# First attention: scores seven quarters ahead in place of eight, maxima rows by one transfer, another order of the first steps

## The reference

```
x = x + L0_attn(layernorm(x))     # 16 heads of 8, differential: x1 - lv*x2, softmax(q k / sqrt 8) v
x = x + L0_ffn(layernorm(x))      # 8 experts, top 2, capacity, 512 wide
x = x + L1_attn(layernorm(x))     # 16 heads of 64, causal, batches of 256
x = x + L1_ffn(layernorm(x))      # 8 experts, top 4, 64 wide, and a shared one
```

## Time and profile before

| | |
|---|---|
| timed runs, median | 1486.77 us (1484.62 to 1487.56) |
| profiled execution | 1496.64 us, span 1495.1 us |
| busy, share of span | PE 96%, DVE 72%, ACT 64%, POOL 50% |
| chain that ended last, by engine | PE 79%, DVE 10%, ACT 5%, issue 2%, POOL 1%, DMA 1% |
| POOL's idle time ahead of `land` (L2441) | 97.0 us, of it 92.2 for the DMA to `dm` |

### The profile page before, as it was taken

One profiled execution on the slowest core, in us unless ns is written; L12 is line 12 of the kernel. 1 busy time (PEld: TensorE's weight loads), 2 busy tenths in 40 slices (PEclk: granted clock), 3 DMA queues, 4 the chain that ended last, 5 costly groups with the idle time before them and its releaser, 6 DMA issues.

```text
span 1495.1 us, 26269 instructions
## 1 busy us (share of the span) xinstructions
PE 1438.5 (96%) x8801; PEld 854.5 (57%) x8801; DVE 1074.0 (72%) x3430; ACT 950.1 (64%) x2448; POOL 744.3 (50%) x1260
## 2 busy tenths in 40 slices
PE   4999999999989999999999999999999999999999
PEld 2434443444437889974565565656565565655666
DVE  5899999999953677647667777777768777674433
ACT  4588888887874333436767777676767767674221
POOL 7434556655554653535636455463636544343322
PEclk9999999999999999999999999999999999999999
DMA  7366655456434565730000000000000000021331
GB/s 136 63 156 134 141 143 147 104 111 150 120 118 149 184 215 183 257 114 15 15 1 14 3 7 11 1 15 2 15 2 9 7 1 2 1 51 37 71 77 51
DMA packets 70601, 113.39 MB, mean 76 GB/s; under 512 B 18858, under 2 KB 35115, under 8 KB 70459
## 3 DMA queue, kind: packets, MB, share of 16 engines
q0 software_dynamic: 33104, 61.73, 17.0%
q1 hardware_dynamic: 36928, 49.19, 11.1%
q10 hardware_dynamic: 434, 0.79, 0.2%
HBM read 71.86 MB, written 39.91 MB: 75 GB/s over the span
## 4 chain that ended last, share of the span: by engine, by line
PE 79%; DVE 10%; ACT 5%; issue 2%; POOL 1%; DMA 1%; ACTq 0%; DVEq 0%; POOLq 0%
PE pS L1396 10%; PE bank L1429 9%; PE bank L1409 8%; PE bank L1240 6%; PE pS L1211 4%; DVE mx L1836 4%; PE bank L1438 4%; PE bank L1381 4%; PE pS L1315 4%; PE bank L1366 4%; PE bank L1329 3%; PE bank L1377 3%; PE pS L1316 3%; PE bank L1477 3%; PE bank L1231 3%
## 5 line engine op out<-in xcount | busy, mean ns | idle before, releaser
L2540 POOL TENSOR_SCALAR ar<-ar,rd 128x512 f32<-128x512 f32 (+3 forms) x512 | 268.2, 537 | 319.0 <-DVE rd L2271 317.1
L1836 DVE TENSOR_REDUCE mx<-pS 128x1 f32<-128x512 f32 x512 | 326.6, 678 | 19.7 <-PE pS L1211 16.2
L1656 ACT ACTIVATE ar<-ar,nm 128x512 f32<-128x512 f32 (+3 forms) x512 | 285.9, 560 | 77.3 <-DVE nm L2262 76.2
L2262 DVE CUSTOM_DVE_ANT_0 ar<-pS,maskf 128x512 f32<-128x512 f32 (+3 forms) x512 | 227.5, 482 | 7.5 <-PE pS L1396 5.7
L1566 ACT ACTIVATE ar<-bank 128x512 f32<-128x512 f32 x342 | 194.2, 598 | 48.6 <-PE bank L1231 41.7
L1409 PE MATMUL bank<-identr,all_r 128*128 128x128 f32 x1280 | 211.7, 287 | 6.0 <-DVE ar L2278 3.9
L1211 PE MATMUL pS<-all_r 64*128 64x512 f32 x512 | 205.9, 478 | 5.6 <-DVE mx L1836 4.7
L1409 PEld LDWEIGHTS bank<-identr,all_r 128*128 128x128 f32 x1280 | 134.4, 140 | 109.7 <-issue 85.6
L1666 ACT COPY ar<-bank 128x512 f32<-128x512 f32 (+3 forms) x256 | 107.1, 418 | 107.3 <-PE bank L1409 104.6
L1396 PE MATMUL pS<-ar 64*128 64x512 f32 (+3 forms) x1024 | 172.9, 456 | 0.8 <-DVE ar L2253 0.8
L1211 PEld LDWEIGHTS pS<-all_r 64*128 64x128 f32 x512 | 85.5, 192 | 127.8 <-DVE mx L1836 102.8
(11 more groups left out here) (306 smaller groups left out, 2632.6 us busy)
## 6 DMA issues: line engine op xcount, KB each, us to landing
rows_in<-zrow SPq DMA_DIRECT2D x16, 1024.0 KB, 5.5
ar<-gd SPq DMA_DIRECT2D x16, 512.0 KB, 6.5
all_r<-dk POOLq DMA_DIRECT2D x56, 128.0 KB, 4.0
dk<-xT SPq DMA_DIRECT2D x21, 256.0 KB, 3.4
dq<-xT SPq DMA_DIRECT2D x16, 256.0 KB, 5.1
rows_out<-ar SPq DMA_DIRECT2D x32, 128.0 KB
all_r<-dq POOLq DMA_DIRECT2D x28, 144.0 KB, 3.8
all_r<-dq POOLq DMA_DIRECT2D x28, 128.0 KB, 3.4
```

What stands on the lines that cost most here:

```text
L1656: S.activation(p, p, ACT.Exp, bias=nm1[:, c:c + 1], scale=-1.0, accum_out=den1[:, c:c + 1]).then_inc(*s_e1.inc(u, a))
L1836: V.tensor_reduce(mx[Gr % 2][:, col:col + 1], bS[n % 3], AX.X, ALU.max, negate=True).then_inc(*s_mx.inc(Gr, c))
L2262: V.tensor_tensor_reduce(pr_[pi][:, 0:w], pS[u % 2][:, 512 * a:512 * a + w], maskf[:, 512 - w:512], -0.125, 3e38, ALU.add, ALU.min, accum_ ...
L2540: G.tensor_scalar(p, p, rd1[:, c + a:c + a + 1], 1.0, ALU.mult, ALU.mult).then_inc(*s_p1.inc(u, a))
```

## The change

It does six things.

1. `AHEAD = 7`: step n has the scores of quarter n+7. The prefill has seven quarters. The loop has 129 steps; `now = n - 1` takes the old step number's place for all side work, so that `beside`, `behind` and `late` stand to the scores as before, and one step later to the exponentials. `parts(1)` is in step 0. Seven steps with exponentials have no scores.
2. `land` and the tensors `dm` are gone. After ScalarE's copy SyncE issues two DMAs from `mT` straight into `qst`. To make that possible `parts` writes `mp` in another order of columns.
3. For the first batch, the first two head pairs' k rows are loaded by SyncE, on a semaphore of their own (`a_sk`).
4. The zero rows of the first operands: GpSimd keeps one half, VectorE takes the other (`zero`, 32x4096), ahead of the first `ln`. `zero_more` is only the load of ones, behind `ln p 1`.
5. `ones_of_v` is cut in two, one after the k projection, one after the first loads.
6. q(1) with its low part, k(1) with its low part, and v(1) come after the quarters 0, 1, 2 of group 1 and after the last, all after group 0. `zero 1` comes ahead of group 0's quarters.

```
+AHEAD = 7
-        if at % 4 == 2 and Gr + 1 < NG:
-            add("land", Gr + 1)
...
-    for unit in (("ones_of_v",), ("ln", "p", 0), ("zero_more",), ("apply", "p", 0), ("ln", "p", 1), ("turn", 0),
-                 ("apply", "p", 1), ("q", 0), ("low", "q", 0), ("k", 0), ("low", "k", 0), ("lam",), ("turn", 1)):
+    for unit in (("ln", "p", 0), ("apply", "p", 0), ("turn", 0), ("q", 0), ("low", "q", 0), ("ln", "p", 1),
+                 ("zero_more",), ("k", 0), ("low", "k", 0), ("ones_of_v", 0), ("apply", "p", 1), ("lam",), ("turn", 1)):
         add(*unit)
     for m in range(8):
         add("stack", 0, m)
+    add("ones_of_v", 1)
     add("v", 0)
-    add("q", 1)
     for m in range(8, 16):
         add("stack", 0, m)
-    add("low", "q", 1)
     add("consts")
-    for n, more in enumerate(([("k", 1)], [("low", "k", 1)], [("v", 1), ("zero", 1)], [])):
-        for unit in quarter(0, n) + more:
+    add("zero", 1)
+    for n in range(4):
+        for unit in quarter(0, n):
             add(*unit)
     add("parts", 0)
-    for n in range(4):
-        for unit in quarter(1, n):
+    for n, more in enumerate(([("shift", 0)], [("q", 1), ("low", "q", 1)], [("k", 1), ("low", "k", 1)], [("v", 1)])):
+        if n < AHEAD - 4:
+            for unit in quarter(1, n):
+                add(*unit)
+        for unit in more:
             add(*unit)
         if n == 0:
-            add("shift", 0)
-            add("land", 0)
             for b in range(2):
                 add("bias_x", b)
             add("ones", 1)
-    add("parts", 1)
+    if AHEAD == 8:
+        add("parts", 1)
...
+    def step(n, now, filled):
+        pieces = {"P": [], "F": filled, "B": []}
+        if n < 4 * NG:
+            for m, j in enumerate(order_of(n // 4, n % 4)):
+                pieces["E%d" % m] = [("exp", n // 4, n % 4, j)]
+        s = n + AHEAD
+        for m, unit in enumerate(quarter(s // 4, s % 4) if s < 4 * NG else []):
+            pieces["S%d" % m] = [unit]
...
+    for n in range(4 * NG + 8 - AHEAD):
+        now = n + AHEAD - 8
...
+        last = taken(behind, b, 4 * g + kb) if now >= 0 else taken(add, "parts", 1)
...
         def shift(Gr):
-            i = Gr % 2
+            b, g, i = Gr // 4, Gr % 4, Gr % 2
             SP.wait_ge(*s_mact.at("shift", Gr))
-            if Gr >= 2:
-                SP.wait_ge(*a_ms[i].at(2 * (Gr // 2)))
-            Q.dma_start(dm[i], mT[i]).then_inc(*a_dm[i].inc())
+            if b >= 2:
+                SP.wait_ge(*st_done(b - 2))
+            for a in range(2):
+                Q.dma_start(qst[b % 2][64 * a + 32:64 * a + 34, 2 * g:2 * g + 2, :].bitcast(F32)
+                            .rearrange("c i (q n) -> c (i q) n", q=4),
+                            mT[i][16 * a:16 * a + 16, :]).then_inc(*a_ms[i].inc())
...
+        def stack(b, m):
+            if b or m not in range(4, 8):
+                return
+            a, n = m // 2 % 2, m % 2
+            SP.wait_ge(*s_za.at(0))
+            SP.wait_ge(*s_zp.at(0))
+            SP.wait_ge(*s_zd.at(0))
+            SP.wait_ge(*a_dk[0].at(3))
+            heads = dk[0].rearrange("(i a) c n -> a c i n", a=2)
+            Q.dma_start(kst[0][64 * a + 16 * n:64 * a + 16 * n + 16, 0:2, :].bitcast(F32),
+                        heads[a][8 * n:8 * n + 16, 0:2, :]).then_inc(*a_sk.inc())
...
+        def zero(i):
+            if i == 0:
+                V.memset(zero_rows(0, 1)[:, 4096:8192], 0.0).then_inc(*s_zd.inc(0))
...
         def zero_more():
-            POOL.wait_ge(*s_rstd.at("p", 0))
-            G.memset(zero_rows(0, 1)[:, 4096:8192], 0.0).then_inc(*s_zp.inc(0))
             ones(0)
...
-            mv_ = mx[i][:, :].rearrange("p (j q) -> p q j", j=4)
+            mv_ = mx[i][:, :].rearrange("p (i a q) -> p a i q", i=2, a=2)
...
-            G.tensor_copy(mp[i][:, :, 0:4].bitcast(F32R), mv_).then_inc(*c_pool.inc())
+            G.tensor_copy(mp[i][:, :, 0].bitcast(F32R), mv_).then_inc(*c_pool.inc())
```

More of the change, by code:

```diff
@@ new lines, in order_of @@
+    def order_of(Gr, kb):
+        return JS if 4 * Gr + kb + AHEAD < 4 * NG else (0, 1, 2, 3)
+    def step(n, now, filled):
[6 more added lines that the diff above has]
+            pieces["S%d" % m] = [unit]
+        if 0 < n < 4 * NG:
+            before = ((n - 1) // 4, (n - 1) % 4)
+            pieces["P"] = [("pv", *before, i) for i in order_of(*before)]
+        if n % 4 == 0 and 0 < n < 4 * NG:
+            pieces["T"] = [("take", n // 4 - 1)]
+        if now >= 0:
+            b, at = now // 16, now % 16
+            pieces["F"] = filled + ([("diff", b - 1)] if filled and b > 0 and at == 2 else [])
+            pieces["B"] = beside(b, at)
@@ L346, in step @@
         return pieces
     filled = []
-    for Gr in range(NG):
+    for n in range(4 * NG + 8 - AHEAD):
+        now = n + AHEAD - 8
+        Gr, kb = now // 4, now % 4
         b, g = Gr // 4, Gr % 4
[L351 to L354, removed]
+        pieces = step(n, now, filled)
+        filled = [unit for of_ in pieces["B"] for unit in emptied(*of_)]
+        last = taken(behind, b, 4 * g + kb) if now >= 0 else taken(add, "parts", 1)
+        if now >= 0:
@@ L355, in schedule @@
             if kb in (2, 3) and g and 2 * (3 * b + g - 1) + kb - 2 < LATE:
                 last += taken(add, "late", 2 * (3 * b + g - 1) + kb - 2, Gr)
[L357 to L367, removed]
@@ L368, in schedule @@
-    for j in order_of(NG - 1):
+        small = [unit for unit in [(kind, tuple(key)) for kind, *key in pieces["F"]] + last if unit[0] in SMALL]
+        for engine, tokens in STEP.items():
+            for token in tokens.split():
+                if engine == "DVE" and token in ".*":
+                    n = 1 if token == "." else len(small)
+                    units.extend((*unit, engine) for unit in small[:n])
+                    small = small[n:]
+                elif token == "D":
+                    units.extend((*unit, engine) for unit in last)
+                else:
+                    units.extend((kind, tuple(key), engine) for kind, *key in pieces.get(token, []))
@@ L369, in schedule @@
+    for j in order_of(NG - 1, 3):
         add("pv", NG - 1, 3, j)
@@ L767, in program @@
     mx = [sb(f"mx{i}", [128, 16]) for i in range(2)]
-    mp = [sb(f"mp{i}", [128, 4, 8]) for i in range(2)]
+    mp = [sb(f"mp{i}", [128, 32])[:, :].rearrange("p (a c i q) -> p a c i q", a=2, c=2, i=2) for i in range(2)]
     mT = [xT4[0:32, 2048 + 128 * i:2176 + 128 * i] for i in range(2)]
@@ L948, in program @@
     a_w0, a_rt, a_cst, a_w1, a_wqk, a_zr, a_zo = (Load(nc, f"a_{n}") for n in ("w0", "rt", "cst", "w1", "wqk", "zr", "zo"))
+    a_sk = Load(nc, "a_first_keys")
     a_zq, a_st0 = Load(nc, "a_zq"), Load(nc, "a_st_first")
-    a_dq, a_dk, a_dm, a_st, a_st_late, a_ones, a_ms = (
-        [Load(nc, f"a_{n}{i}") for i in range(2)] for n in ("dq", "dk", "dm", "st", "st_late", "ones", "ms"))
+    a_dq, a_dk, a_st, a_st_late, a_ones, a_ms = (
+        [Load(nc, f"a_{n}{i}") for i in range(2)] for n in ("dq", "dk", "st", "st_late", "ones", "ms"))
     a_eo = [Load(nc, f"a_eo{i}") for i in range(NEO)]
@@ L1152, in sync_program @@
         begin()
-        mine = {"late": late, "q": q_rows, "k": k_rows, "shift_": shift, "clear": clear,
+        mine = {"late": late, "stack": stack, "q": q_rows, "k": k_rows, "shift_": shift, "clear": clear,
                 "outward": outward, "wqk": qk_weights, "gturn": gates_out,
@@ L1218, in shift @@
             PE.wait_ge(*s_id.at("identf"))
-            M.transpose(misc[0:32, 0:128].bitcast(F32R), mp[i][:, :, :].rearrange("p q c -> p (q c)").bitcast(F32R),
+            M.transpose(misc[0:32, 0:128].bitcast(F32R), mp[i].rearrange("p a c i q -> p (a c i q)").bitcast(F32R),
                         identr[:, :]).then_inc(*s_full.inc("shift", Gr))
@@ L1779, in apply, with ones_of_v @@
             ins.then_inc(*s_norm.inc(stage, b))
-        def ones_of_v():
-            for i in range(2):
-                V.memset(ar2[:, 2048 * i:2048 * i + 2048], 0.0).then_inc(*c_dve.inc())
-                after()
-                V.memset(vst[i][:, :, :, 8:9], 1.0).then_inc(*s_v1s.inc(i))
+        def ones_of_v(i):
+            V.memset(ar2[:, 2048 * i:2048 * i + 2048], 0.0).then_inc(*c_dve.inc())
+            after()
+            V.memset(vst[i][:, :, :, 8:9], 1.0).then_inc(*s_v1s.inc(i))
+        def zero(i):
+            if i == 0:
+                V.memset(zero_rows(0, 1)[:, 4096:8192], 0.0).then_inc(*s_zd.inc(0))
         def low_part(what, b, src):
@@ L2313, in vector_program @@
                 "likely_inverse": likely_inverse, "likely_times": likely_times, "chosen_count": chosen_count,
-                "place_first": place_first, "apply": apply, "ones_of_v": ones_of_v, "low": low,
+                "place_first": place_first, "apply": apply, "ones_of_v": ones_of_v, "zero": zero, "low": low,
                 "v_": v_rows, "lam": lam_, "consts": consts,
@@ L2376, in ln @@
             if (stage, b) == ("p", 0):
-                after()
```

(5 more changed lines are left out.)

27 lines of the change are left out of this document (13 added, 14 removed).

## The result

The changed kernel is slower. Four timed runs gave 1507.12 us (1503.90 to 1510.35), against 1487.16 (1484.62 to 1487.61) for four of the kernel before: ratio 1.0139, 95% interval 1.0125 to 1.0152. The forecast was 1483.6, its range ended at 1487.2. The profiled execution took 1509.67 us (13.0 more than before) with a span of 1508.4 (13.3 more). That is less than the 20.0 us between the medians: the profiled execution of before stood 9.5 us above its median, this one 2.6 above.

A forecast was written before the change was run, and what follows sets the result against it. The prediction took TensorE to bound the steady steps, leaving gains only at the front and last steps. Terms -0.5 - 3.2 + 0.5 = -3.2 us from 1486.77 gave 1483.6, range 1478.8 to 1487.2.

The forecast's parts named there:

- Maxima rows sent direct: Each group's first exponential: landing mostly 2.0 us after ScalarE's copy, three or four groups at the limit; cost 0.5 us.
- Rival (c): Direct landings decide, slower: some 15 of 31 groups lose about 0.7 us each, +6 in sum, 1493; chance 0.07.
- The normalisation: Front: one memset fewer on VectorE's path and `apply` without GpSimd's memset; q and k projections 3.8 us earlier.
- The first scores: Front: keys loaded by SyncE land at 23.6 to 24.5, scores from 24.4, first reduction 25.8, 4.3 us won.
- The order of the first steps: Seven quarters ahead: first exponential's matmul at 50.0 (49.2 to 51.2), 2.8 us earlier, of which 0.5 stays.
- The rise of the clock: First steps: TensorE goes from 1.2 to 2.4 GHz 5 us after the first exponential's matmul, bounds 3 and 7.
- rival (b): The front's lead is eaten: the 0.5 us gain becomes +1.3, sum -0.4, 1486.4; chance 0.28.
- The end and the saved step: Attention's end: seven steps without scores in place of eight, 3.2 us saved, between 2.70 and 4.06.
- Rival (a): The slow clock at attention's end disappears: 7.2 us gained there, 1479.6; chance 0.15.
- The rule on VectorE and GpSimd's descriptors: Front: VectorE's memset and `apply` could delay GpSimd's q loads by at most 3.0 us, sum -2.3; left out of the sum.
- Sum: Whole kernel: -0.5 at the front, -3.2 at the last steps, +0.5 for landings, -3.2 us in all.

The follow-up runs named there:

- paced kernel: Changed kernel plus GpSimd waiting for the next group's maxima rows to land before its next-batch loads: 1493.42 us, ratio to before 0.9990.
- both waits: Changed kernel; GpSimd waits for the maxima rows' landing and holds late first-batch loads until SyncE's keys land: 1491.92 us, 0.9981; again 1495.65, 0.9970.
- the projections moved: Changed kernel with GpSimd's wait for the maxima rows and q(1), k(1), v(1) back among group 0's quarters: 1496.34 us, ratio to before 0.9981.
- the 4 KB form: Changed kernel, maxima rows in four 4 KB transfers, not two of 8 KB: 1552.34 us, 1.0326; with GpSimd's landing wait too, 1504.37.

## Why the prediction was wrong

**The step that failed** is "Maxima rows sent direct": "Cost 0.5, bounds 0 and 4". Measured: 14.9 us of waits and up to 11.9 of clock behind them. Its reading of the room was right: 2.7 to 5.6 us after the copy, measured mostly 3.3, 4.0, 4.5 and 5.0 by place in the batch. What it took for the landing was not. It read 1.74 and "5.3 at worst" off GpSimd's side of `land`, and took the 5.3 for an exception. Those numbers were taken under the wait that the change removes. While `land` stood in GpSimd's list, its bulk loads of the next batch could not be issued just ahead of the maxima rows; the paragraph says itself that `land` goes, and calls GpSimd's 6.71 us of waiting "off the path". It counted what the freed engine stops doing and not what it starts to do earlier. Even an undisturbed landing takes 2.6 and not 2.0, but at 2.6 no group stalled in the paced kernel; the 14 crowded ones decided.

**Rival (c)**, landings that decide, had the right sign and mechanism, and a chance of 0.07. It put 0.7 us on 15 groups, 1493; there were nine at 1.65 us on average (14.9 in all), and the clock on top, which no rival priced. Its condition, a mean landing of about 3.7 us, was met: 18 groups at 2.6 and 14 at about 5 make 3.7. The evidence for it was in the same views: the four q loads beside the hop.

**The normalisation**: right. Statistics at 5.21 in place of 5.52, `apply` 1.11 in place of 4.18, q projection at 10.57 in place of 13.89.

**The first scores**: wrong. The keys' landing was put at 23.6 to 24.5, from one load's 2.4 and an allowance of 0.9; it came at 29.3. The allowance was for the late q rows, yet GpSimd's issues from 20.4 to 24.7 were eight late loads of 192 to 216 KB. With these held back the forecast was met: 24.8 for the score and 25.9 for the reduction, against 24.4 and 25.8.

**The order of the first steps**: first exponential "50.0", measured 54.35. The first reduction was 4.4 late (30.20 against 25.8), and from there to the exponential it took 24.15 us where the prediction's count gives 24.2. But this agreement held only with late keys. With the scores on time the exponential still came at 53.8 to 54.8, since group 1 then waits for the late rows (the prediction took no stall, with 2 us as the bound; first score of group 1 at 39.4 with both waits, 4.75 of it waiting for them). The rise of the clock, put at 5 us after the exponential's matmul with bounds 3 and 7, came 1.6 us after it, at 56.0, and gave some of that back. The prediction sets step 3 beside the old step 2: its PV group stands at 63.2 against 60.9, 2.3 behind where 0.5 ahead was forecast. That is rival (b), the front's lead eaten, and more than its 1.3.

**The end and the saved step**: "3.2". By the same pairing, from the PV group of step 120 (before) or 121 (seven quarters) to the end of the last one, before took 29.9 us, after 22.8, the kernel with both waits 27.6 in one profile and 23.3 in the other. The clock stood at its lower level for 10.2, 3.4, 10.2 and 0 us of these. At the same 10.2 us the saving is 2.3, and 2.3 again between the paced kernels with eight and with seven quarters and the projections moved (31.4 and 29.1, 13.7 us low in each). So the step is worth 2.3 at a like clock, and the 3.2 was too much. Rival (a), the slow clock of the end gone, did not settle into a rule: it is partly true of after's profile, while the paced kernel's has 23.9 us at 0.50 there and one of the two with both waits none. The two profiles with both waits are of one kernel, and put the price of 10.2 us at the lower level at 4.3 us. Timed runs of that kernel lay between 1489.4 and 1499.3 us in the first measurement; how much of this is the clock of the last steps is not shown.

**The rule on VectorE and GpSimd's descriptors** ("DMA: Bandwidth & Descriptors", SWDGE vs HWDGE vs iDMA, of the Trainium skill) would, by the prediction's estimate, have pushed the q loads by up to 3.0 us. In after the eight issues from 18.10 took 4.55, 0.57 each, beside `apply` and the second of the two memsets, against 0.5 for k rows before: no delay of that size. And VectorE's memset of 32x4096 ran beside GpSimd's of the same size (3.47 us from 1.71, 3.51 from 2.17) without either being slowed (2048 columns took 1.76). So the part of the estimate that stood on VectorE's memset, 1.9 of the 3.0, has no row for it and this one against it.

**Sum.** Forecast -3.2; without the two crowds the change measures -0.1% (paced) to -0.3% (both waits), -1.5 to -4.5 us. That this lies around the forecast is luck. In the second profile with both waits attention ends 3.6 us earlier than before: the front is 1.8 behind (forecast: 0.5 ahead), the last steps give 2.3 (forecast: 3.2), and the 118 steps between them take 358.7 us in place of 361.8, a gain of 3.1 for which the prediction had no term.

**What stays open.** The 3.1 us of those 118 steps: with eight quarters and the wait they take 361.1, so most of it belongs to the seven quarters (sixteen steps take 49.4 us in place of 49.8), but no run shows by what. Nor is it shown why eight quarters without the wait (1.0039, slower than before beyond its interval) and with it (1.0017) cost anything, when no group stalled in either profile; the two differ by 0.2%, with intervals that overlap.

## What to carry to other kernels

A wait on an engine off the critical path may be what keeps its bulk DMAs behind somebody's small urgent one. Before taking such a wait away, list what that engine issues next, how many KB it is, and which transfer will then stand behind it; and keep the wait when only the transfer changes (here it cost nothing that could be measured). When a margin is shortened by one step and a latency is changed in the same edit, measure the latency's worst case without the thing that the edit removes.

## What the runs showed of the hardware

**A small transfer waits for the bulk of another queue.** Packets by microsecond around group 2, KB moved by GpSimd's queue and 512-byte packets by SyncE's:

```
after (issued 73.43)       72: 164 KB   73: 138   74: 128   75: 134   76: 216   77: 32 KB, 32 packets   78: 4
paced (issued 74.09)       72: 176 KB   73: 174   74: 36    75: 0, 16 packets   76: 0, 16 packets
```

All 32 packets of the 16 KB start when the bulk has nearly run out: the first at 77.08, 3.65 us after the issue, in place of 1.25. Once begun, each transfer is through in under half a microsecond. The Trainium skill ("DMA: Bandwidth & Descriptors", Queues, rings and completion order) says that each DMA engine goes round the queues that have work for it and drains a whole packet of one before it switches, and that a packet typically holds 9 to 17 descriptors, each the order for one piece of data. The pieces of 512 B and 2 KB in this trace are not such packets: most 2 KB pieces took 0.17 to 0.35 us, so by an estimate from the Trainium skill's 9 to 17 one turn of the bulk is 1.5 to 6 us long, and the 3.65 us fit within it. That asks for a packet to reach over several loads, since 128 to 144 KB over 16 engines are 4 to 5 pieces each. The trace does not show where a packet ends, so it does not tell long turns from a queue that is served first. The same page of the Trainium skill ("Why a DMA increments its semaphore by 16 and not by 1") gives the number of engines as the largest number up to 16 that divides the outermost sizes of both sides: two here, eight for the 4 KB form. The completion packets agree (2 and 8), but the experiment shows that it isn't what bounds.

**The clock falls within a busy stretch.** In a list that is otherwise 98% busy, stops of 2.47, 1.88, 2.13 and 1.97 us (groups 2, 11, 15 and 19) were each followed by 3.4 or 6.8 us at 1.2 GHz; those of 1.76 and 1.85 (groups 23 and 27) and the shorter ones by none. The length of the stop alone does not decide it: in the kernel with seven quarters and the old hop, a stop of 1.70 us (group 5) was followed by 3.4 us at 1.2 GHz, and stops of 2.23 and 2.21 (groups 2 and 26) by none. In the paced kernel, without such stops, the clock stayed at 2.4 GHz from 59.0 to 427.6.
